# Token classes finished beside the last pieces, W2 read through a register, W1 rounded on ScalarE

## What is computed

```python
x = x + conv(layernorm(x), Wq, Wk, Wv, Wp, ...)     # spiking attention, leaky states over 4 time steps
t = x.reshape(6272, 128)                             # tokens
n = layernorm(t)
gate = softmax(n @ Wg)                               # 8 experts
topv, topi = top_k(gate, 2)
topv = topv / (sum(topv) + 1e-6)
for e in range(8):
    h = gelu(n @ W1[e] + b1[e])                      # 128 -> 512
    ye = h @ W2[e] + b2[e]                           # 512 -> 128
    out += ye * score_of_e
result = t + out
```

## Time and profile before

| | us |
|---|---|
| median of 3 runs | 499.63 (498.39 to 501.27) |
| the profiled execution | 499.74 |
| its span, first to last instruction | 497.7 |
| TensorE busy in the span | 344.0 |
| VectorE busy | 383.6 |
| ScalarE busy | 289.8 |
| POOL busy | 216.0 |

### The profile page before, as it was taken

The page is one execution under the profiler, slowest core; times in us unless marked ns, Lnnn a source line. Parts: engine busy times, 40 slices in busy tenths (PEclk is TensorE's granted clock), DMA queues, the critical chain, the costliest instruction groups (busy, mean ns, idle before and its releaser), DMA issues.

```text
span 497.7 us, 9750 instructions
## 1 busy us (share of the span) xinstructions
PE 344.0 (69%) x2628; PEld 287.1 (58%) x2628; DVE 383.6 (77%) x1344; ACT 289.8 (58%) x684; POOL 216.0 (43%) x233
## 2 busy tenths in 40 slices
PE   2665959556475577543297879899999999999000
PEld 2343526334243254321186878799999999999000
DVE  5588797999979969999788777866766666664296
ACT  3367565467654674545376575466566666667083
POOL 3000000027174027373554777777776655655300
PEclk9976565857657755675589999999999999999655
DMA  6911010102122004343421224432332222221399
GB/s 166 293 43 20 10 23 10 24 25 67 29 62 57 10 26 104 83 107 85 89 81 45 88 80 139 117 93 86 91 94 68 76 70 72 71 62 39 124 349 307
DMA packets 62197, 43.36 MB, mean 87 GB/s; under 512 B 29105, under 2 KB 56793, under 8 KB 62144
## 3 DMA queue, kind: packets, MB, share of 16 engines
q1 hardware_dynamic: 53696, 28.85, 22.4%
q0 software_dynamic: 6720, 12.97, 8.3%
q10 hardware_dynamic: 1728, 0.94, 0.6%
HBM read 22.09 MB, written 19.91 MB: 84 GB/s over the span
## 4 chain that ended last, share of the span: by engine, by line
DVE 43%; PE 41%; issue 5%; ACT 4%; DMA 2%; DVEq 2%; ACTq 1%; POOLq 0%; POOL 0%; SPq 0%
PE PS L1387 15%; DVE U L1146 6%; DVE VV L1138 6%; DVE H_all L1128 5%; PE PS L1374 4%; PE PS L1244 4%; PE PS L1375 4%; PE PS L1376 4%; DVE stats L744 3%; PE PS L1320 3%; DVE X L1204 2%; PE PS L1359 2%; DVE spikes L1156 2%; ACT XN L564 2%; DVE X L1208 2%
## 5 line engine op out<-in xcount | busy, mean ns | idle before, releaser
L520 POOL DMA_INDIRECT by_expert<-XG,place x98 | 99.1, 1011 | 187.7 <-DVE place L905 159.6
L505 POOL DMA_INDIRECT by_token<-osp,target x112 | 112.1, 1001 | 61.2 <-issue 60.9
L1387 PE MATMUL PS<-w_now,hid 128*128 128x128 f32 x896 | 108.8, 275 | 0.0
L1387 PEld LDWEIGHTS PS<-w_now,hid 128*128 128x128 f32 x896 | 104.6, 192 | 0.0
L630 ACT ACTIVATE hid<-PS,b1c 128x256 f32<-128x256 f32 x224 | 88.1, 475 | 15.0 <-PE PS L1376 11.9
L1374 PE MATMUL PS<-rows_high,w_high 128*128 128x256 f32 x224 | 68.8, 307 | 3.2 <-DVE rows_low L1006 2.4
L639 ACT ACTIVATE w_now<-W_s 128x512 f32 x56 | 35.5, 634 | 56.2 <-PE PS L1387 55.0
L1375 PE MATMUL PS<-rows_low,w_high 128*128 128x256 f32 x224 | 63.8, 285 | 0.0
L1376 PE MATMUL PS<-rows_high,w_low 128*128 128x256 f32 x224 | 63.6, 284 | 0.0
L1244 PE MATMUL PS<-xT,wT 128*128 128x392 f32 x96 | 62.5, 784 | 0.7 <-ACT xT L575 0.7
L1138 DVE SCALAR_TENSOR_TENSOR VV<-H_all 128x196 f32<-128x196 f32 (+2 forms) x152 | 50.0, 329 | 2.9
(11 more groups left out here) (178 smaller groups left out, 552.9 us busy)
## 6 DMA issues: line engine op xcount, KB each, us to landing
rows_in<-by_expert SPq DMA_DIRECT2D x56, 130.0 KB
X<-in_x SPq DMA_DIRECT2D x7, 448.0 KB, 6.2
out<-X SPq DMA_DIRECT2D x7, 448.0 KB, 5.8
xT<-by_token SPq DMA_DIRECT2D x3, 896.0 KB, 7.5
xT<-in_L_ffn_W SPq DMA_DIRECT2D x4, 512.0 KB
by_token<-osp,target POOLq DMA_INDIRECT x112
H_all<-by_token SPq DMA_DIRECT2D x2, 896.0 KB, 11.6
W_s<-by_token SPq DMA_DIRECT2D x2, 896.0 KB, 11.4
```

The costliest lines, as they stand in the source:

```text
L505: pool.indirect_dma_start(by_token, bass.IndirectOffsetOnAxis(ap=target[b][:, a:a + 1], axis=0), rows_out[b][:, a, :], None, bounds_check= ...
L520: pool.indirect_dma_start(by_expert, bass.IndirectOffsetOnAxis(ap=place[g % SENDING][:, k, r:r + 1], axis=0), XG[g % SENDING][:, r, :], No ...
L1387: m = pe.matmul(PS[:, down_bank(j), a * 128:a * 128 + 128], hid[b % 2][:, hb, a * 128:a * 128 + 128], w2_now[b % 2][:, hb * C:hb * C + C], ...
```

## The change

Four edits:

- **W1 is rounded on ScalarE.** `set_up` on VectorE no longer makes `w1_high`; ScalarE's new `round_w1(j + 2)` does, behind `gelu(j)`, and VectorE's subtraction waits for it (`w1_rounded`). `w2_now` and its copy are gone.
- **W2 is read in place.** `down` on TensorE loads the piece's expert into a register and addresses `W2_s` with it.
- **Token classes.** The later pieces are cut by class: rows that were placed when tile 30 had been reached, then those up to tile 42, then the rest, and within a class by expert. With 3 classes of 8 experts the tables of steps 10 to 14 have 24 columns instead of 8 (33 by 24 for the pieces, 24 by 24 for the sums). So all rows of the tiles before 30 are finished after piece 36, and those before 42 after piece 48.
- **Six row groups are finished in the loop.** SP gathers groups 0 to 2 between fetch(43) and fetch(44), group 3 behind fetch(50), groups 4 and 5 after the last fetch, into three buffers; VectorE and ScalarE weigh a group in two parts, of four and of three tiles, at the steps in `WEIGH_AT`; group 6 stays for the end, in two parts. The exponentials move to piece 11 and the scores to step 32; the two scalings by the norm move from step 25 to step 10.

```diff
+    FINISHED = [GATE_CUTS[EARLY_GATES], 42]
+    CLASSES = len(FINISHED) + 1
+    SEGS = CLASSES * E
+    finished_after = [cut + E * (ROWS - 1) // ROWS for cut in FINISHED]
+    WEIGH_AT = {42: (0, 0, 4), 43: (0, 4, R), 44: (1, 0, 4), 45: (1, 4, R), 46: (2, 0, 4), 47: (2, 4, R),
+                48: (3, 0, 4), 49: (3, 4, R), 52: (4, 0, 4), 53: (4, 4, R), 54: (5, 0, 4), 55: (5, 4, R)}
+    GATHER_FROM = finished_after[0] + 6
+    EXPONENTS_AT = 11
+    SCORES_AT = 32
+    LAST_CUT = 4
...
             for j in range(EARLY, PIECES):
                 fetch(j)
-            for b in range(OUTS):
-                sp.wait_ge(rows_sent[b], 16 * HALVES * (PIECES // OUTS))
-            sp.wait_ge(down_done, PIECES + AHEAD)
-            for g in range(G):
-                sp.dma_start(shares[g], by_token_v[:, R * g:R * g + R]).then_inc(shares_in[g], 16)
+                if j == GATHER_FROM:
+                    sent(finished_after[0])
+                    for g in range(3):
+                        gather(g)
+                elif j == GATHER_FROM + 7:
+                    store(0)
+                    gather(3)
+                elif j == GATHER_FROM + 10:
+                    store(1)
+            store(2)
+            sent(finished_after[1])
+            gather(4)
+            gather(5)
+            store(3)
+            store(4)
+            sent(PIECES)
...
+            def round_w1(j):
+                e = expert_of_gelu[j] = act.value_load(piece_expert[0:1, j:j + 1], min_val=0, max_val=E - 1)
+                act.wait_ge(up_done, HB * (j + 1))
+                nc.scalar.activation(w1_high[j % 2][:], w1_rows[:, bass.ds(e * HID, HID)],
+                                     ACT.Copy).then_inc(w1_rounded, 1)
...
             def piece_on_act(j):
                 if j == 0:
                     act.wait_ge(b1_copied, 1)
-                set_w2(j)
                 gelu(j)
+                if j + AHEAD < PIECES:
+                    round_w1(j + AHEAD)
...
             def set_up(j, b):
-                v.wait_ge(up_done, HB * (j + 1))
-                v.tensor_copy(w1_high[b % 2][:], w1).then_inc(w1_set, 1)
+                e = expert_of[j] = v.value_load(piece_expert[0:1, j:j + 1], min_val=0, max_val=E - 1)
                 if j >= AHEAD:
                     rows_up(j, b)
-                v.wait_ge(w1_set, 2 * j + 1)
+                v.wait_ge(w1_rounded, j + 1)
...
+                elif k == SCORES_AT:
+                    gate_shares()
+                if k - 1 in WEIGH_AT:
+                    add_second(*WEIGH_AT[k - 1])
+                if k in WEIGH_AT:
+                    weigh_first(*WEIGH_AT[k])
...
             def down(j, b, last=False):
+                first = pe.value_load(piece_expert[0:1, j:j + 1], min_val=0, max_val=E - 1)
...
-                                      w2_now[b % 2][:, hb * C:hb * C + C], start=(hb == 0), stop=(hb == HB - 1))
+                                      w2_rows[:, bass.ds(first * HB * C + hb * C, C)], start=(hb == 0), stop=(hb == HB - 1))
```

More of the change, by code:

```diff
@@ L442, in _, with sent, gather, store @@
             scattered_until(GATES)
+            def sent(pieces):
+                for b in range(OUTS):
+                    n = len(range(b, pieces, OUTS))
+                    sp.wait_ge(rows_sent[b], 16 * HALVES * n)
+            def gather(g):
+                if g >= 3:
+                    sp.wait_ge(out_ready, 2 * (g - 2))
+                sp.dma_start(shares[g], by_token_v[:, R * g:R * g + R]).then_inc(shares_in[g], 16)
+            def store(g):
+                sp.wait_ge(out_ready, 2 * g + 2)
+                sp.dma_start(out_v[:, R * g:R * g + R, :], X[:, R * g:R * g + R, :]).then_inc(stored, 16)
@@ L455, in _ @@
+            sp.wait_ge(out_ready, 2 * LAST + 2)
+            sp.dma_start(out_v[:, n:TILES, :], X[:, n:TILES, :]).then_inc(stored, 16)
+            sp.wait_ge(stored, 16 * (G + 1))
         @block.gpsimd
@@ L671, in _ @@
                     copy_y(slot - 1)
+                if slot == BLOCKS:
+                    for j in range(AHEAD):
+                        round_w1(j)
                 for k in late_steps[1:2]:
@@ L680, in _, with weigh_second @@
                     piece_on_act(k)
+            def weigh_second(g, r0, r1):
+                act.wait_ge(last_in if g == LAST and r0 else shares_in[g], 16)
+                for r in range(r0, r1):
+                    n = R * g + r
+                    m = nc.scalar.activation(shares[g][:, r, 1, :], shares[g][:, r, 1, :], ACT.Copy,
+                                             scale=score[:, n, 1:2])
+                m.then_inc(second_weighed, 1)
             for j in range(max(STEP_AT.values()) + 1, PIECES):
                 piece_on_act(j)
+                if j == EXPONENTS_AT:
+                    gate_exponents()
                 if j == PAD_AT - DEEP:
@@ L690, in _ @@
                                   pad_rows[:]).then_inc(padded, 16)
+                elif j in WEIGH_AT:
+                    if not any(at < j for at in WEIGH_AT):
+                        act.wait_ge(shares_ready, 1)
+                    weigh_second(*WEIGH_AT[j])
                 elif j - PAD_AT + DEEP == E // 2:
@@ L906, in rank_rows @@
                 elif stage == 5:
+                    cut = GATED[g][1]
+                    if cut in FINISHED or cut == TILES:
+                        k = FINISHED.index(cut) if cut in FINISHED else CLASSES - 1
+                        do(v.tensor_tensor(filled_at[:, k, :], small[:, n, :], filled[:], ALU.add))
                     v.tensor_tensor(filled[:], small[:, n, :], filled[:], ALU.add).then_inc(filled_ready, 1)
@@ L1107, in later_starts, with weigh_first, add_second @@
                                 ALU.min).then_inc(pieces_ready, 1)
                 v.wait_ge(pieces_ready, 2)
+            def weigh_first(g, r0, r1):
+                v.wait_ge(last_in if g == LAST and r0 else shares_in[g], 16)
+                for r in range(r0, r1):
+                    n = R * g + r
+                    do(v.scalar_tensor_tensor(X[:, n, :], shares[g][:, r, 0, :], score[:, n, 0:1], X[:, n, :],
+                                              ALU.mult, ALU.add))
+            def add_second(g, r0, r1):
+                rows = X[:, R * g + r0:R * g + r1, :]
+                steps.wait(steps.count)
+                v.wait_ge(second_weighed, 2 * g + (2 if r0 else 1))
+                v.tensor_tensor(rows, rows, shares[g][:, r0:r1, 1, :], ALU.add).then_inc(out_ready, 1)
```

174 lines of the change are left out of this document (102 added, 72 removed).

## The result

| | before | after |
|---|---|---|
| median, us | 499.34 (498.39 to 501.27) | 483.04 (480.68 to 486.72) |
| ratio, 95% interval | | 0.967 (0.964 to 0.970) |
| profiled execution | 499.74 | 480.68 |
| its span | 497.7 | 478.7 |
| TensorE / VectorE busy | 344.0 / 383.6 | 341.7 / 366.6 |

The forecast was 482.8. The profiled execution of after is the shortest of its four, so the traces differ by 19.0 us and the medians by 16.3. A part of this is in the slots: the up products of piece 0 begin at 245.54 us here and at 247.97 in before. Of these 2.4 us, 0.9 are the change (two roundings fewer in step 0); the other 1.5 lie ahead of step 0, which VectorE reaches at 242.52 and not 244.02, and are this run's: in the eight later kernels with the same slots as after, the up products of piece 0 begin at 245.74 to 248.15. Sizes are therefore compared from one point of a trace to the next.

What follows compares the result with a forecast made beforehand. TensorE was taken to bound the kernel until 461 us, DMA after it. From 499.74 us, terms -18.8 - 1.0 + 1.1 + 1.5 + 0.3 + 0 = -16.9 gave 482.8 us; forecast 479 to 485.5 (0.66), 8-in-10 range 478.0 to 490.0.

Steps and rivals of the forecast that it cites:

- The tail: After the piece loop: only row group 6 is left, read in two parts; end 478.9 instead of 497.7, -18.8 us.
- The early steps: Steps before piece 16: roundings leaving VectorE give -3.3 us, wider class tables in steps 10 to 14 cost +2.3; -1.0 us.
- POOL moves forward with VectorE and stays out of the way: POOL's unbroken run from 269.54 us starts on VectorE's number, so it moves forward by about 2.1 us.
- Scores in step 32: Five dependent operations of gate_shares plus an exposed register load in step 32: one stall, +1.1 us.
- The table loads of the exponents at piece 11: ScalarE's table load and the one back to GELU, 1.28 us each, fall in idle time at piece 11: 0.
- Weighing: Beside pieces 42 to 55: VectorE's four-product chain overruns by 0.3 us in five steps, +1.5 us (0.7 to 4).
- my upper end of 3.7: Weighing steps: if durations add without overlap, VectorE needs 3.7 us a step and the cost is 4 us.
- The gathers on SP's queue: fetch(44) to fetch(49) stand behind three gathers; fetch(44) lands about 414.7 against 414.4: +0.3 us, zero to 2.
- the pair: Gathers of groups 4 and 5, issued 5.8 us after step 49's addition, land 449.3, wanted 450.0: 0, up to 1 us.
- the rival of colliding transfers: Gathers and stores share 16 DMA engines with fetches and sends; fetch(44) 3 us late, later transfers too: 487 us; chance 0.11.
- The register read: TensorE's register load and addresses ahead of each piece's down products are hidden: 0 us, range 0 to 0.75 a piece.
- The sum: Whole kernel: -18.8 - 1.0 + 1.1 + 1.5 + 0.3 + 0 = -16.9 from 499.74, giving 482.8 us.

Runs made afterwards that it cites:

- weight edits alone: The kernel before with only W1 rounded on ScalarE and W2 addressed through a register; 498.97 us, ratio 0.998.
- classes alone: The changed kernel with both weight edits undone, keeping classes, weighing in the loop and short tail; 491.01 us, ratio 0.985.
- the twelve buffers: 12 result buffers instead of 8: in the kernel before with the two weight edits 493.40 us; in the changed kernel 482.59 us.
- all four remedies: The changed kernel with 12 result buffers, scores spread over steps 32 to 36, gather(2) and store(2) issued later; 478.06 us, ratio 0.9585.

## Why the prediction was right, step by step

**The tail: right, 1.7 us too small.** Said -18.8, measured -20.5 from the issue of the first gather to the end. Issue to last addition was 7.84 in my working and is 7.89. The term that was mis-sized is the end behind the last addition: I took 4.2 of the 4.35 us of before, and it was 2.45. The traces tell what the difference is. The last store of before landed 3.93 us after its issue, that of after 2.05. About 1.0 of this is the size: a store of 0.46 MB on its own (after's at 458.80) lands in 3.04 us, and after's last has three tiles and not seven, 0.20 MB. The other 0.9 is a queue: before, two stores were still in flight when the last was issued at 493.38 and landed at 494.68 and 495.99, and DMA moved 345 GB/s though no gather was left:

```profile
492.00:495.00 3.00, 0.00 (x0) 0.00 (x0) 1.32 (x2) 0.00 (x0) 0.00 (x0) 0.50 1.15 345
```

That queue went into the loop with the other groups; my working kept it at the end.

**The early steps: said -1.0, measured -3.2 at piece 20, of which about 1.5 is this run's early slots.** The rounding brought more than I took: from piece 0 to 10, 48.9 us became 45.4, 3.5 us less (3.1 with the weight edits alone), and 0.9 in step 0, together 4.4. I had 4.2 in full and struck it down to 3.3 for other engines; that was too much. The tables came out near: an operation on 792 columns took 0.98 us as worked out, and between pieces 10 and 16 after loses 1.9 us, where I said 2.3. But the terms that I listed for them add up to 5.8 us and not to the 4.7 that I wrote; measured it is 4.6 (classes alone, pieces 10 to 16), so the figure was right and its working wasn't. What failed is the sentence that POOL moves forward with VectorE and stays out of the way. Its unbroken run began 4.0 us earlier (265.54 and not 269.54), and the 12 scatters of the last group ended 3.2 us earlier, but VectorE came 5.9 earlier to piece 10. POOL's pace of 1.27 to 1.3 us a transfer then sets the time, and the up products of piece 20 come 3.2 us earlier, as the scatters do. In the trace of before, the wait of 0.60 us at 326.59 was the sign: a wait that is already there takes up what is won ahead of it, here 5.8 of 7.0 us. The weight edits alone and the twelve buffers show this.

**Scores in step 32: right.** Said 1.1, measured 1.23. My own rows give 0.35 for the exposed register load (0.75 where 0.4 stood) and not the 0.2 that stands in the sum; with it the working gives 1.26. The table loads of the exponents at piece 11 cost nothing that shows.

**Weighing: the mechanism right, the size off by a factor of three.** Said 1.5 us for five steps of four products, 0.3 each; measured 0.13 at pieces 46, 48 and 50, some 0.5 with what the others add. I had put the chain of step 42 at 3.48 us as if an addition of the second shares stood in it, and its first step has none: from the bias addition (413.32) to the end of rows_low (416.19) it took 2.87 us, below the 3.15 that are free. Where both stand in a step the chain was 3.34 us (step 44, 421.03 to 424.37), so the overrun was 0.2 by the same sum, and piece 46 came 0.13 late. With the rounding left on VectorE (classes alone), the same stretch runs at 3.79 us, near my upper end of 3.7.

```profile
413.32 0.42 DVE L1115 TENSOR_TENSOR osp<-PS,b2b 128x256 f32<-128x256 f32 x1 [1.16 <-PE PS L1529]
413.66 0.21 DVE L1107 SCALAR_TENSOR_TENSOR target<-rows_in,piece_rank 128x2 int32<-128x2 f32 x1
413.79 1.13 DVE L1239 SCALAR_TENSOR_TENSOR X<-H_all,score,X 128x128 f32<-128x128 f32 x4
414.84 0.42 DVE L1094 CAST rows_high<-PS 128x256 fp32r<-128x256 f32 x1
415.18 0.68 DVE L1086 TENSOR_TENSOR w_low<-xT,w_high 128x512 fp32r<-128x512 f32 x1
415.77 0.42 DVE L1099 TENSOR_TENSOR rows_low<-PS,rows_high 128x256 fp32r<-128x256 f32 x1
```

**The gathers on SP's queue: the place wrong, the size 2.5 us too small.** Said 0.3 (0 to 2) for the first three and 0 (up to 1) for the pair. Measured 0.85 at piece 43, inside the range; and +1.97 at piece 54, outside it. The step that failed is "issued 5.8 us after step 49's addition, lands at 449.3". The issue was about right (443.95, 5.4 us behind that addition); from it to 449.3 would have been 5.3 us, about the 5.2 that group 0's gather took with no store ahead of it. My working has no term for store(2), which stands behind fetch(55) in the same queue and was issued 0.75 us ahead of the gather. The rows were in use at 451.3. Of the rival of colliding transfers this is the true part, at 2.8 us where I had priced 4.

**The register read: right, at 0.** That it had room for a second load, and not for a third, bears the reason out too: the load is hidden, and not cheap. Whether the up products alone make the room stays open, as said above. For the size the Trainium skill ("DMA: Bandwidth & Descriptors", the section on latency and other measured facts) gives a floor of about 600 ns for a tensor_load; the 0.60 to 0.65 us per load, checks included, agree. Fully exposed it would have cost 40 x 0.6 = 24 us, more than the gain.

**The sum.** Terms as measured: -20.5 - 3.2 + 1.2 + 0.9 + 0.5 + 2.0 = -19.1, the span's -19.0. Against the prediction's -16.9 the tail is 1.7 and the early steps 2.2 better, the other terms together 1.7 worse. That is 2.2 us more than forecast. The medians differ by 16.3, and the forecast fits them to 0.3 us by luck: its errors have both signs, and after's four runs lie between 480.68 and 486.72, with the profiled one at the low end.

## What to carry to other kernels

When an engine ahead of a throughput-bound queue is made faster, look first for a wait on that queue that is already in the trace, however short: here it took 5.8 of the 7.0 us won, and more buffers, not more speed, released it, at the price of a few more waits at the end. Moving a tail's transfers into a loop costs by its place in the queue, so count every store and fetch ahead of each gather, and put what nobody waits for behind what somebody does. Spare time counts step by step, not in the sum: five short dependent operations in one step stalled TensorE for 1.2 us, and one in each of five steps for nothing.

## What the runs showed of the hardware

- TensorE's sequencer hid two register loads a piece in 3.43 us of matmuls, and not a third: one and two loads cost 0, three 0.13 and four 0.78 us in each of pieces 20 to 33, and 11 and 39 us of the whole time. By estimate it had room for 1.6 to 1.8 us, at 0.60 to 0.65 a load.
- A gather of 0.52 MB was in use 4.43 us after its issue with nothing ahead of it; one of 0.92 MB took 7.3 us behind a store of 0.46 MB and 5.5 us with the store behind it.
- A store of 0.20 MB landed 2.05 us after its issue and one of 0.46 MB in 3.04; with two stores still in flight ahead of it, one of 0.46 MB took 3.93.
- POOL issued indirect transfers, scatters and sends alike, mostly every 1.27 to 1.30 us and at times 1.4 to 2.0, whatever waited for them.
- Four stalls of 0.9 to 2.0 us, each behind another engine or queue, could be taken away together: of 5.5 us in after's trace 5.3 were gone from these places with all four remedies in. The whole time fell by 4.4 (ratios) to 5.0 us (medians).
